# Unread f32 products on TensorE in slots 7 to 19 of the last cross attention and slots 87 to 93 of its closing chain

## What is computed

```python
x = x + L2_attn(layernorm(x));  x = x + L2_xattn(layernorm(x), ctx)
x = x + L2_ffn(layernorm(x));   x = x + L3_attn(layernorm(x))
x = x + L3_xattn(layernorm(x), ctx);  x = x + L3_ffn(layernorm(x))

def L2_xattn(query, key, value, w_concat):       # 16 heads of 8 features
    scores = einsum('bhqd,bhkd->bhqk', q, k) / sqrt(8)
    ctx = einsum('bhqk,bhkd->bhqd', softmax(scores), v)
    return ctx.transpose(0, 2, 1, 3).reshape(B, S, 128) @ w_concat.T

def L2_ffn(x, w_gate, w_up, w_down):             # operands rounded to FP4 in blocks of 16
    h = silu(fp4_linear(x, w_gate)) * fp4_linear(x, w_up)
    return fp4_linear(h, w_down)

def L3_attn(h, queries):                         # no softmax
    q = einsum('bnd,ed->bne', h, queries)
    return einsum('bnm,bmd->bnd', einsum('bne,bme->bnm', q, h), h)
```

## Time and profile before

| | us |
|---|---|
| median of 3 runs | 1234.09 |
| lowest and highest | 1230.27 and 1236.34 |
| the profiled execution, its time | 1232.24 |
| the profiled execution, its span | 1230.9 |
| PE busy in it | 1020.5 (83%) |
| DVE busy in it | 796.3 (65%) |
| ACT busy in it | 604.1 (49%) |

### The profile page before, as it was taken

The page is one execution under the profiler, slowest core; times in us unless marked ns, Lnnn a source line. Parts: engine busy times, 40 slices in busy tenths (PEclk is TensorE's granted clock), DMA queues, the critical chain, the costliest instruction groups (busy, mean ns, idle before and its releaser), DMA issues.

```text
span 1230.9 us, 20157 instructions
## 1 busy us (share of the span) xinstructions
PE 1020.5 (83%) x7777; PEld 558.1 (45%) x7777; DVE 796.3 (65%) x1984; ACT 604.1 (49%) x1018; POOL 252.5 (21%) x309
## 2 busy tenths in 40 slices
PE   5777689998999974687877899999568788779999
PEld 4233233343776642345542333566323233447767
DVE  7786877731316468878768872767688877664412
ACT  2456345566335346678745677323026456333342
POOL 2933400000000234687631000001120001000000
PEclk9789879999999985568676999999758789779999
DMA  8334140000000310076105103500102100100000
GB/s 306 96 80 99 53 169 2 3 2 1 1 1 1 103 35 1 27 207 130 33 26 198 33 3 52 93 1 14 39 26 87 45 1 2 35 1 1 1 9 9
DMA packets 35586, 62.33 MB, mean 51 GB/s; under 512 B 5059, under 2 KB 25364, under 8 KB 33892
## 3 DMA queue, kind: packets, MB, share of 16 engines
q1 hardware_dynamic: 33828, 58.64, 16.8%
q10 hardware_dynamic: 1664, 2.41, 0.7%
HBM read 42.95 MB, written 16.65 MB: 48 GB/s over the span
## 4 chain that ended last, share of the span: by engine, by line
PE 58%; DVE 27%; ACT 5%; issue 4%; POOL 3%; DMA 2%; SPq 1%; DVEq 0%; POOLq 0%; ACTq 0%
PE ps_s L902 10%; PE ps_e L892 9%; PE ps_v L694 6%; DVE mx L1896 6%; PE ps_e L610 4%; PE ps_e L625 4%; PE ps_s L640 3%; DVE ps_s L1892 2%; PE ps_e L996 2%; ACT work L1419 2%; DVE mx L1886 2%; PE ps_s L983 2%; DVE stats L1834 1%; DVE xn L1852 1%; DVE work L2371 1%
## 5 line engine op out<-in xcount | busy, mean ns | idle before, releaser
L1419 ACT ACTIVATE work<-ps_e 128x512 f32<-128x512 f32 x448 | 243.6, 597 | 146.1 <-PE ps_e L610 144.7
L2650 POOL TENSOR_TENSOR rstd<-rstd,halves 128x2 f32<-128x2 f32 x52 | 36.7, 706 | 688.6 <-DVE rstd L1839 688.4
L1896 DVE TENSOR_REDUCE mx<-ps_s 128x2 f32<-128x1024 f32 x128 | 153.9, 1222 | 26.7 <-PE ps_s L640 25.3
L640 PE MATMUL ps_s<-ctx_stack,q_stack 49*128 49x512 bf16 (+1 forms) x384 | 126.3, 443 | 47.1 <-DVE mx L1896 34.2
L1526 ACT ACTIVATE work<-ps_s,keep 128x512 f32<-128x512 f32 x136 | 93.1, 687 | 140.3 <-PE ps_s L902 137.4
L610 PE MATMUL ps_e<-q_stack,ctx_stack 52*128 52x256 bf16 (+1 forms) x768 | 143.8, 294 | 8.7 <-ACT work L1419 2.6
L694 PE MATMUL ps_v<-work,vaug 128*32 128x256 f32 x1536 | 130.4, 415 | 4.8 <-ACT work L1407 4.8
L892 PEld LDWEIGHTS ps_e<-ffn_w,work 128*128 128x128 f32 x960 | 117.8, 196 | 21.0 <-issue 19.9
L902 PE MATMUL ps_s<-xnT,ffn_w 128*128 128x512 f32 x240 | 119.0, 620 | 3.6 <-ACT work L1526 3.6
L892 PE MATMUL ps_e<-ffn_w,work 128*128 128x128 f32 x960 | 119.6, 279 | 0.8 <-DVE x L2082 0.8
L2092 DVE SCALAR_TENSOR_TENSOR x<-ps_e,gates,x 128x128 f32<-128x128 f32 x128 | 38.9, 346 | 122.8 <-PE ps_e L892 119.8
(11 more groups left out here) (381 smaller groups left out, 1852.1 us busy)
## 6 DMA issues: line engine op xcount, KB each, us to landing
q_stack<-q_scr SPq DMA_DIRECT2D x32, 192.0 KB
ffn_w<-in_L0f_w SPq DMA_DIRECT2D x1, 4608.0 KB, 15.8
ffn_w<-in_L1f_w SPq DMA_DIRECT2D x1, 3456.0 KB, 14.1
q_scr<-parts SPq DMA_DIRECT2D x16, 192.0 KB, 2.1
c_scr<-ffn_w SPq DMA_DIRECT2D x12, 256.0 KB, 7.6
kx_scr<-ffn_w SPq DMA_DIRECT2D x12, 256.0 KB, 4.2
ctx_stack<-kx_scr SPq DMA_DIRECT2D x2, 1536.0 KB
ctx_stack<-c_scr SPq DMA_DIRECT2D x2, 1536.0 KB
```

The lines of the kernel that those rows point to most:

```text
L640: return pe.matmul(ps_s[i][:, parity, :], q_stack[p0:p0 + n_rows, b, pair, part * P:(part + 1) * P], ctx_stack[p0:p0 + n_rows, pair, b * S ...
L1419: act.activation(pt[:, parity, :, :].rearrange("p k q -> p (k q)"), bank[f"e{parity}"], ACT.Exp).then_inc(exped, 1)
L1896: m = dve.tensor_reduce(mx[:, b, :, pair, part], ps_s[i][:], AX, ALU.max, negate=True)
```

## The change

A helper `spin(n, name)` is added to PE's program. It claims the bank and issues n products of two slices of `keep` into the second half of the bank. Nobody reads them, they signal nothing, and each later use of the bank begins anew (`start=True`). It is called in two places: three products in each of X2's slots 7 to 19, ahead of that slot's scores; and four products in every pass of the chain's loop body in slots 87 to 93, ahead of that batch's step.

```diff
+        def spin(n, name=None):
+            for bank_name in (name,) if name else ("e0", "e1"):
+                if name:
+                    claim(name)
+                if bank_name not in free:
+                    for _ in range(n):
+                        pe.matmul(bank[bank_name][:, S:2 * S], kp("L1a_out"), kp("L1x_qT", 0, S), start=True, stop=True,
+                                  skip_group_check=True)
+                    return
+
...
             if t == LEAD[use] + 4:
                 pe.wait_ge(d_vload, 16 * {X0: 1, X1: 2, X2: 3}[use])
+            if use == X2 and EARLY_X2 + 2 <= t < LEAD[use]:
+                spin(3, "e1")
             if t < STEPS[use] + LEAD[use]:
                 pair_step(use, t, tile)
...
         def chain(slot):
             tile = ring if slot < TAIL0 else window_tile
             for b, at in chain_steps(slot):
+                if 87 <= slot < TAIL0:
+                    spin(4, "e1")
                 if at == 7:
```

## The result

| | before | after |
|---|---|---|
| median, us | 1232.18 (4 runs, 1226.91 to 1236.34) | 1266.53 (4 runs, 1264.37 to 1268.06) |
| profiled execution, its time | 1232.24 | 1267.76 |
| its span | 1230.9 | 1266.4 |

The changed kernel is slower: the ratio after to before is 1.0287, with a 95% interval of 1.0251 to 1.0323. The forecast was 1263 us in a range of 1252 to 1276.

A forecast was written before the change was run, and what follows sets the result against it. PE was taken to bound most of the kernel (58% of the chain of waits, DVE 27%), though half idle in both places; 35.4 - 2.8 - 1.7 + 0 = +30.9 on 1232.24 gave 1263 us, range 1252 to 1276.

The forecast's parts named there:

- The price of a product: Each added f32 product of 128x256 takes PE 0.43 us at the full clock, 0.86 at the low one.
- The fourth rival: Filler nearly free at about 0.11 us a product, chain stretch 17.7 us, kernel faster at about 1224 us; 3%.
- point of decision: Chain: 20.4 us of room over 112 products, 0.18 us each, as the price below which filler would pay.
- Slots 87 to 93: Closing chain up to the routing: 112 products and PE's own work take 53.6 us in place of 18.2, +35.4.
- The head of the routing: From routing to third up product: 20 products ahead cover DVE's FP4 rounding, leaving a head of 3.7 us, -2.8.
- The clock at the second up products: Up products at 1102.37 us ran at the low clock; full clock worth 0 to -3.4, half taken, -1.7.
- Slots 7 to 19: X2's slots with 39 products: delay near 2.3 us, returned later, sum 0, with -5 and +8 as ends.
- The return of 1.4 us: After slot 19, PE at full clock halves the second L1047 and DVE's wait for it goes, -1.4.
- the second: Rival: the clock stays low in slots 7 to 19, +21.5, about 1284 us; 5%.
- the third: Rival: the filler runs in the chain at the low clock, +87, 1315 us; 2%.
- the fifth: Rival: the additions are not what the numbers say, for instance 28 in the chain, no loss.
- the first: Rival: full clock lasts through X2's slots 20 to 40 and the experts' first products, another -1.7 and -5, 1256 us; 15%.

The follow-up runs named there:

- chain_bf16: Changed kernel without the products in slots 7 to 19 and with the 112 chain products in bf16 instead of f32: 1232.64 us, ratio 0.9993 to before.
- gap_fill: Changed kernel with its fillers replaced by 21 f32 products in the chain, only where PE waits: 1231.2 us, ratio 1.0007 to before.
- chain_28: Changed kernel with one f32 product instead of four per chain pass, 28 in all, none in slots 7 to 19: 1231.99 us, ratio 0.9993 to before.
- gap_fill_slots_1: gap_fill plus one f32 product per slot in X2's slots 7 to 19: 1230.0 us, ratio 1.0005 to before.
- fill_76: Kernel before plus only 5 f32 products in slot 76, in PE's wait ahead of the transposes of L3's norm: 1232.01 us, ratio 0.9998.
- slots_only: Changed kernel without the chain's products, only the 39 f32 products in slots 7 to 19: 1236.44 us, ratio 1.0015 to before.
- slots_1: Changed kernel with one f32 product per slot instead of three in slots 7 to 19, none in the chain: 1229.15 us, one run.
- slots_2: Changed kernel with two f32 products per slot instead of three in slots 7 to 19, none in the chain: 1238.57 us, one run.
- chain_only: Changed kernel without the products in slots 7 to 19, only the 112 f32 products in slots 87 to 93: 1263.45 us, ratio 1.0246 to before.
- fill_all: gap_fill plus the 5 products of fill_76 and 14 behind the routing, 40 f32 products in waits: 1225.72 us, ratio 0.9950 to before.

## Why the prediction was right, step by step

**The price of a product** (0.43 us) was read from L565's start-to-start distance and holds to the digit. The fourth rival, filler at a quarter of it, is what chain_bf16 made true, and with it the loss vanished; the rival's point of decision, 0.18 us, lies between the two measured prices of 0.11 and 0.43. But at 0.11 the rival counted on a gain of 8 us, 6.7 of it in the chain, and the run gave none (1232.64 against 1233.69, at most 5.3 us by the interval). Its trace has the returns, 2.2 us at the routing's head and 3.3 at the second up products. What the rival had wrong is the stretch to the routing, 17.7 us without any wait: it took 20.64, because 2.92 us of waits stayed (0.54, 1.00 and 1.38), and the closing is down by 3.1 us only (43.45 for 46.58). The room for filler is not one sum; each wait takes only what stands ahead of it.

**Slots 87 to 93** were put at 53.6 us for 18.2, +35.4; measured 53.11, +34.9. The count of 112, PE without waits and the clock at 1.00 are all in the trace.

**The head of the routing**, -2.8: measured 3.72 us for 6.50, -2.8, and the table load and the gelus follow as described. gap_fill is the counter-check: without the 20 products ahead of the routing the 3.3 us of DVE's rounding are back.

**The clock at the second up products**, -1.7 as half of 3.4: this low stretch was gone in the changed kernel, and the part from the third up product to L565 went from 20.87 to 17.54 us, -3.3. The other traces show it as a draw: there in chain_28, gap_fill_slots_1 and fill_76, gone in chain_bf16 and gap_fill, which have no more filler behind the routing than those, and gone in slots_only, which has none after slot 19. Taking half of it was an even bet, and the changed kernel's trace drew the whole.

**Slots 7 to 19** are the step that was mis-sized. I put the delay at 2.3 us, all of it at the start; it is 4.8 in the changed kernel, 3.9 in slots_only. The price of a slot was taken as 3 x 0.43 + 0.2 = 1.5 us of PE; it is 1.81, since three f32 products between bf16 scores take 1.50 and not 1.29, and the scores 0.32 and not 0.2. At 1.5 DVE's mean of 1.75 us a slot would have stayed the longer one; at 1.81 PE is. slots_1 and slots_2 show the same limit from below. The return of 1.4 us at the second L1047 didn't come in the changed kernel either: PE waited 1.65 us for DVE shortly ahead of it, and it ran for 2.93 us at the low clock, as long as before (2.87). In slots_only it ran for 1.56 us. So this was a draw as well, and the sum of 0 for this place was 3.5 to 4.8 us too low, the one with the 1.31 us of the table's third row and the other without. (PE's own work here, scaled from the window, is 13.0 us and not 13.1, which changes nothing.)

**The sum** of 30.9 us stands against 35.5 between the two profiled times, of which 3.25 lie ahead of slot 7 and are not the change's, and against 34.4 between the medians. The terms of the chain gave 30.9 and measured 28.8 (34.9 - 2.8 - 3.3); the slots gave 0 and measured 3.5 (4.8 - 1.3, with the 1.3 inside the spread of that stretch). The one is 2.1 us too high and the other 3.5 too low, so the sum, 32.3 us measured in these terms, lies closer than its parts, and that is luck. chain_only and slots_only, in their own comparisons, are 29.8 and 2.8 us above before. PE's busy time grew by 56.9 us (1020.5 to 1077.4), where some 50 were announced. Of the rivals, the second and the third (low clock under the filler) are excluded by the granted clock, 0.91 over slots 7 to 18 and 1.00 in the windows of the chain; the fifth by the 302 records; the first (the clock stays up beyond the additions) came true in the experts' first products and not behind slot 20, where the clock fell at 917.5.

## What to carry to other kernels

Filler on TensorE did raise the clock here, but it is work like any other: it is free only inside a wait, and its length at the full clock must be smaller than the wait, group by group. Count how often the loop body with the filler runs, since 28 products cost nothing here and 112 cost 29 us, and price the filler by its data type, since f32 cost four times what bf16 did. A clock that looks better in the profile, 1.00 for 0.69 here, proves nothing about the time, and a stretch must be compared with several traces of unchanged code before a low stretch in one of them is called a loss.

## What the runs showed of the hardware that I had not expected

A wait ahead decides the clock for longer than it lasts, and full occupation doesn't always bring it back. In the kernel before PE is busy nearly without a break from 1044 to 1053 us, mostly with bf16 products of 52 rows and f32 products of 32 columns, and stays at the low level, behind a wait of 2.49 us:

```profile
1041.78 0.41 PE L558 MATMUL ps_m<-keep,xn 128*128 128x128 f32 x2 [2.49 <-DVE xn L1852]
```

```profile
1044.00:1053.00 9.00, 8.80 (x56) 3.38 (x58) 3.64 (x13) 4.89 (x10) 0.00 (x0) 0.50 0.01 2
```

With 5 f32 products of the full 128x128 array inside the wait ahead of it, the same work stays at the full level in fill_76 (and in fill_all, which has them too):

```profile
1043.65 2.32 PE L561 MATMUL ps_m<-keep 128*128 128x256 f32 x10
1046.22 0.44 PE L569 MATMUL ps_m<-keep,xn 128*128 128x128 f32 x2 [0.24 <-DVE xn L1867]
```

```profile
1048.00:1056.00 8.00, 7.59 (x74) 3.27 (x74) 5.28 (x19) 5.89 (x12) 0.03 (x1) 1.00 0.01 2
```

The Trainium skill, "TensorE: Matmul & The Clock Gate", section "What's actually happening", says that the gate follows how busy PE has been recently; the row at 1044 shows PE busy for 8.80 of 9 us with the gate at half, and there the trace does not agree, if busy is what the profile counts as busy. No run here shows why.

Going from the scores to f32 products and back costs time too. Three f32 products ahead of scores take 1.39 us behind the f32 projection and 1.40 behind transposes, and 1.50 behind other scores, where 3 x 0.43 would be 1.29, as these rows of the changed kernel show:

```profile
888.38 2.32 PE L1059 MATMUL ps_s<-keep,xnT 128*128 128x384 f32 x4
890.53 1.46 PE L560 MATMUL ps_e<-keep 128*128 128x256 f32 x6
891.92 0.39 PE L650 MATMUL ps_s<-ctx_stack,q_stack 49*128 49x512 bf16 x2
892.24 1.56 PE L560 MATMUL ps_e<-keep 128*128 128x256 f32 x6
893.74 0.39 PE L650 MATMUL ps_s<-ctx_stack,q_stack 49*128 49x512 bf16 x2
```

The change of type alone is not what costs: in chain_bf16 four bf16 products on the whole array between f32 ones take 0.43 us (1069.00 to 1069.43), 0.11 each, as in a row of 24. What else sets the scores apart, such as their 49 rows, no run separates.
